# A sorted-expert feed-forward kernel: gathers paced by their own landings, and row transposes moved on VectorE

## The reference

```python
ys = cond_1024 / sqrt(512)
d = rsqrt(einsum('bi,io->bo', ys * ys, weight * weight) + 1e-8)
xf = einsum('bsi,io->bso', x * ys[:, None, :], weight) * d[:, None, :]       # conditioned input
top1 = argmax(softmax(xf @ gate_w.T), axis=-1)                               # one of 2 experts
masked = xf[None] * one_hot(top1).T[:, :, None]
h = relu(einsum('end,edh->enh', masked, w1) + b1[:, None, :])                # experts
routing = (einsum('enh,ehd->end', h, w2) + b2[:, None, :]).sum(axis=0)
shared = relu(xf @ sw1 + sb1) @ sw2 + sb2                                    # shared network
out = x + routing + shared
```

## Time and profile before

| | |
|---|---|
| median of 3 runs | 1408.37 us (1406.78 to 1408.86) |
| the profiled execution, its own time | 1408.37 us |
| span of that execution in the trace | 1406.6 us |
| PE busy | 1367.4 us (97%) |
| DVE busy | 1004.5 us (71%) |
| ACT busy | 679.7 us (48%) |
| POOL busy | 364.2 us (26%) |
| DMA, mean over the span | 238 GB/s |

### The profile page before, as it was taken

How to read it: one execution, slowest core, us unless ns; L and a number is a source line. 1 busy time by engine, 2 the same in 40 slices (tenths; PEclk the granted TensorE clock), 3 DMA queues, 4 the chain that set the end, 5 groups by cost and what they waited for, 6 DMA issues and landing times.

```text
span 1406.6 us, 17366 instructions
## 1 busy us (share of the span) xinstructions
PE 1367.4 (97%) x5990; PEld 1126.0 (80%) x5990; DVE 1004.5 (71%) x1424; ACT 679.7 (48%) x988; POOL 364.2 (26%) x328
## 2 busy tenths in 40 slices
PE   9999999999989999899999999999999999897997
PEld 7888888888868788787888888888888887785886
DVE  7979967667788967966557878777897758453331
ACT  4456644545455544665666444444564445231220
POOL 0000005544636544250000000000000032354884
PEclk9999999999999999999999999999999999998999
DMA  6967475776877578653668887978787899997762
GB/s 206 285 244 223 181 250 189 252 231 251 268 257 260 209 255 272 229 181 129 213 224 281 262 281 251 290 254 272 258 250 244 273 291 320 290 298 178 215 163 33
DMA packets 243449, 334.54 MB, mean 238 GB/s; under 512 B 71760, under 2 KB 106576, under 8 KB 243088
## 3 DMA queue, kind: packets, MB, share of 16 engines
q1 hardware_dynamic: 216592, 299.58, 64.7%
q0 software_dynamic: 21248, 30.30, 9.8%
q10 hardware_dynamic: 5520, 3.54, 0.8%
HBM read 201.25 MB, written 149.29 MB: 249 GB/s over the span
## 4 chain that ended last, share of the span: by engine, by line
PE 86%; DMA 6%; DVE 4%; issue 2%; POOL 1%; ACT 1%; POOLq 0%; DVEq 0%; ACTq 0%; SPq 0%
PE bank L2015 39%; PE bank L2093 30%; PE bank L2122 8%; PE bank L1943 6%; DMA rows<-xf_scratch,quad_tab 1%; DMA y_rows<-x_rows,tab 1%; DMA hin<-hidden_scratch 1%; DMA out<-y_rows,tab 1%; DMA hin<-expert_hidden 1%; DVE vb L1512 1%; PE bank L2034 1%; DVE xw L1448 0%; DMA y_rows<-sorted_rows_out 0%; PE bank L2135 0%; DVE hl L1479 0%
## 5 line engine op out<-in xcount | busy, mean ns | idle before, releaser
L2015 PE MATMUL bank<-xw,w_hi 128*128 128x512 f32 x1792 | 555.9, 392 | 14.3 <-DVE vb L1512 12.2
L2093 PE MATMUL bank<-hl,w_hi 128*128 128x512 f32 x1344 | 414.4, 389 | 2.4 <-DVE hl L1479 2.2
L2015 PEld LDWEIGHTS bank<-xw,w_hi 128*128 128x128 f32 x1792 | 337.9, 189 | 86.8 <-DVE vb L1512 13.8
L1479 DVE TENSOR_TENSOR hl<-hin,hl 128x512 fp32r<-128x512 f32 x400 | 265.1, 686 | 197.5 <-ACT hl L1037 189.9
L1037 ACT CAST hl<-hin 128x512 fp32r<-128x512 f32 x400 | 244.6, 621 | 323.0 <-PE bank L2093 185.1
L2015 PE MATMUL bank<-xw,w_lo 128*128 128x512 f32 x896 | 350.4, 391 | 0.0
L2093 PEld LDWEIGHTS bank<-hl,w_hi 128*128 128x128 f32 x1344 | 251.8, 188 | 56.5 <-issue 3.5
L2093 PE MATMUL bank<-hl,w_lo 128*128 128x512 f32 x672 | 261.4, 389 | 0.0
L2015 PEld LDWEIGHTS bank<-xw,w_lo 128*128 128x128 f32 x896 | 169.3, 189 | 35.7
L1061 ACT ACTIVATE vb<-bank,b 128x512 f32<-128x512 f32 x192 | 130.2, 688 | 115.9 <-PE bank L2015 92.7
L882 POOL DMA_INDIRECT rows<-xf_scratch,quad_tab x128 | 129.6, 1012 | 150.4 <-PE bank L2015 105.2
(11 more groups left out here) (199 smaller groups left out, 1337.1 us busy)
## 6 DMA issues: line engine op xcount, KB each, us to landing
hin<-hidden_scratch SPq DMA_DIRECT2D x168, 512.0 KB
hidden_scratch<-vb SPq DMA_DIRECT2D x120, 512.0 KB
hidden_scratch<-vt SPq DMA_DIRECT2D x48, 512.0 KB
hin<-expert_hidden SPq DMA_DIRECT2D x32, 512.0 KB
w_new<-w_shared SPq DMA_DIRECT2D x52, 256.0 KB, 5.4
expert_hidden<-vb SPq DMA_DIRECT2D x24, 512.0 KB
ring<-x_cols SPq DMA_DIRECT2D x32, 256.0 KB
xf_scratch<-xo SPq DMA_DIRECT2D x32, 256.0 KB, 4.8
```

Source lines behind the costliest of these rows:

```text
L1479: nc.vector.tensor_tensor(hl[:, n % HL, 1, :], hin[:, n // 2 % LOADS, n % 2, :], hl[:, n % HL, 0, :].bitcast(F32), ALU.subtract).then_inc( ...
L2015: last = nc.tensor.matmul(up_bank(u, UP_BANK[c])[p][:], w[:, DOWN_W[c], pair, part], xw[:, c, x, k, :], start=(c in FRESH and n == 1), sto ...
L2093: last = nc.tensor.matmul(bank[p][:], w[:, DOWN_W[c], i, part], hl[:, n % HL, h, :], start=(i == 0 and q == 0), stop=(i == PAIRS - 1 and q ...
```

## The change

Three edits in the up stage.

1. POOL: gather j no longer waits for a count of PE's parts. Instead gathers 8, 16 and 24 each wait until the chunk before them has landed (`rows_sorted`); the first gather waits for `xw_lo` alone.
2. ACT: the cast of operand 0 (`block_hi(s, 0)`) waits for all four flips in place of two.
3. DVE, for blocks 4 to 7: flips 0 and 1 now open group 2 of the block before, flip 2 takes the place where flip 0 stood, flip 3 the place where flip 1 stood, and group 3 has none.

```diff
-GATHER_AT = [9 + 6 * j // 5 for j in range(JW)]
...
                 pool.wait_ge(xw_lo, STEPS * s)
                 for j in range(JW):
-                    pool.wait_ge(up_mm, PER_GROUP * GROUPS * (s - 1) + GATHER_AT[j])
+                    if j > 0 and j % (JW // FLIPS) == 0:
+                        pool.wait_ge(rows_sorted[j // (JW // FLIPS) - 1], DMA * JW // FLIPS * (s - BLOCKS + 1))
                     if (s - 1) * GROUPS == LOOSE_UP[0] and j == JW // FLIPS:
                         pool.wait_ge(loose_up_done, 2)
...
-                act.wait_ge(x_flip, FLIPS * s + (2 if c == 0 else FLIPS))
+                act.wait_ge(x_flip, FLIPS * (s + 1))
...
                 if g == 2 and s < UPS - 1:
-                    for i in range(FLIPS if s < BLOCKS - 1 else 0):
+                    for i in range(FLIPS if s < BLOCKS - 1 else 2):
                         flip(s + 1, i)
                 if more:
                     block_lo(s + 1, 0)
-                    if s >= BLOCKS - 1:
-                        flip(s + 1, 2)
-                        flip(s + 1, 3)
                     x_sum_of(s + 1, 0)
...
                 if g == 2 and BLOCKS - 1 <= s < UPS - 1:
-                    flip(s + 1, 0)
+                    flip(s + 1, 2)
                 add(u, vt1, 5, 4, 0)
...
                 if g == 2 and BLOCKS - 1 <= s < UPS - 1:
-                    flip(s + 1, 1)
+                    flip(s + 1, 3)
```

## The result

| | median | profiled execution | span | TensorE busy | TensorE idle |
|---|---|---|---|---|---|
| before | 1407.57 us (1404.79 to 1408.86, 4 runs) | 1408.37 | 1406.6 | 1367.4 | 39.2 |
| after | 1424.27 us (1419.37 to 1424.89, 4 runs) | 1425.69 | 1423.9 | 1370.1 | 53.8 |

The ratio is 1.0113, with a 95% interval of 1.0091 to 1.0135: the change makes the kernel slower by 1.1%, 17 us. The forecast was 1407.0 with a range up to 1423, so the measured median lies 1.3 us above the range, and the likeliest case was wrong.

The account below looks back on a forecast made before the run. TensorE, busy for 97% of the span, was taken as the bound, with at most 16.4 us of stops to win. Block ends changed by -0.3, -0.3, -1.0 and +0.2, so -1.4 from 1408.37: 1407.0 us, range 1393 to 1423.

Parts of the forecast that it names:

- the likeliest case: The prediction's own forecast for the whole kernel: 1407.0 us, its own range 1401 to 1412, chance 0.5.
- Start of the gathers: First gather of each block on POOL: gain 0 in block 3, 0.9 us earlier in blocks 4 and 6, block 5 unchanged.
- The pace on POOL: Gathers 1.31 us apart inside a chunk plus three landing waits W, making F earlier by 1.1 to 2.1 us.
- W: Landing wait on POOL, from a chunk's last gather issue until its landing is seen: taken as 3.7 us.
- F: Start of flip 3 on DVE, set by the last landing: forecast at 394.9, 475.5, 558.7 and 637.3 in blocks 3 to 6.
- The four last waits: Waits from last gather issue to flip 3 in blocks 3 to 6: 6.4, 4.6, 5.7 and 2.45 us, taken as unchanged.
- What a late F costs: At block ends, step 4 may start at F + 4.1 us and DVE's third addition ends at F + 11.3.
- The tail and the second stop: After flip 3, first sum 2.2 us later; PE stops at steps 4 and 6, 1.4 us clock loss partly hidden.
- Flips 0 to 2 cost nothing: On DVE, flips 0 and 1 opening group 2 cost nothing if rows are there; no DMA wait at flips 0 to 2.
- The sum: PE's lateness at the ends of blocks 3 to 6 changes by -0.3, -0.3, -1.0 and +0.2: -1.4 us.
- Slow landings: Rival: bursts queue deeper on POOL; W = 5.0 gives 1423, up to 1444; 11 us per us of W from 4.1; chance 0.23.
- Quick landings: Rival: W and last waits near 2.45 us, all PE block-end stops gone, 1392 us; chance 0.17.

Follow-up runs that it names:

- e1: Kernel before with the change's landing waits on POOL alone, flips and ACT's wait as before: 1421.30 us, ratio 1.0104.
- e7: Kernel before with gathers in bursts of eight set by PE's count (gathers 0, 8, 16, 24 at counts 9, 19, 29, 38): 1407.62 us, ratio 1.0002.
- The parts alone: e1 and e2, each the kernel before with only some of the change's edits: ratios 1.0104 and 1.0047.
- e2: Kernel before with the moved flips and ACT's longer wait alone, gathers still paced by PE's count: 1412.91 us, ratio 1.0047.
- e11: Kernel before with gathers at PE counts 7 + 8j/7 in place of 9 + 6j/5: 1395.13 us, ratio 0.9918.
- e9: Kernel before with gathers at PE counts 9 + 8j/7 in place of 9 + 6j/5: 1400.50 us, ratio 0.9952.
- e4: Kernel after with the three landing waits on POOL left out, so no pacing: 1473.16 us, ratio 1.0485.
- e13: Kernel after with one landing wait in place of three, at gather 24 for chunk 2: 1458.66 us, ratio 1.0369.
- e6: Kernel after with landing waits two chunks behind (gather 16 for chunk 0, gather 24 for chunk 1): 1471.99 us, ratio 1.0486.
- e8: Kernel before with one gather at every PE count (9 + j): 1410.65 us, ratio 1.0018.
- e10: Kernel after with one landing wait in place of three, gather 16 waiting for gathers 8 to 15: 1397.50 us, ratio 0.9945.
- e12: Kernel before with one landing wait at gather 16 in place of all PE counts, old flips: 1451.85 us, ratio 1.0324.

## Why the prediction failed, by its own steps

**Start of the gathers: right in kind, misread in block 3.** There the first gather is released by DVE's `xw`, as forecast, but at 337.84 in place of 339.8. Before, the cast ended at 338.83 and the gather's row names PE as releaser, so PE's count held it for another 1.0 us; after, the cast itself starts at 336.34 in place of 337.61. Those 2 us were a gain that I had at 0. In block 5 the side path, which the forecast took as the limit, no longer binds: gather 8 is released at 530.70 by the landing of the chunk before it.

**The pace on POOL: the failed step.** W was mis-sized: 3.7 forecast, 4.5 measured, and the interval inside a chunk 1.31 forecast, 1.43 measured. By the prediction's own formula that is 28 x 0.12 + 3 x 0.8 = 5.8 us a block. Block by block, from first gather to F: 58.6 for 55.1 forecast in block 3, 63.5 for 53.3 in block 4, 54.7 for 51.2 in block 6. W was built from 3.1 us for the bytes and 0.55 from there until the waiting engine went on. In the kernel after, at the twelve landing waits, the last packet of the gathers' queue ends 2.1 to 6.1 us after the chunk's last issue, 4.0 on the mean, and POOL goes on 0.6 to 1.1 us behind it, 0.8 on the mean. Less the 0.3 of an issue that is 0.5. So the second part was right and the time of the bytes was short by 0.9. Two causes can be seen. The readings were a little early: taken to the packet that completes each chunk's bytes, the 16 of the kernel before give 3.4, not 3.1. And they came from gathers paced at about 1.6 us; in e1, which has bursts and landing waits, the bytes take 4.1 us. How much of that is the burst is open, since in e7, with the same bursts and PE's count, the same reading gives 3.5 for the first three chunks of a block (3.2 before). The longest wait, to 461.04 in block 4, shows what the gathers meet. The DMA queues of the kernel after from 456 to 458 us, then from 459 to 461:

```profile
q1 hardware_dynamic: 384, 0.76, 99.2%
...
q0 software_dynamic: 8, 0.00, 0.7%
```

```profile
DMA packets 17, 0.03 MB, mean 16 GB/s; under 512 B 2, under 2 KB 2, under 8 KB 17
```

For 2 us SP's queue (q1) fills the 16 engines and the gathers' queue (q0) moves 8 packets; its last one ends at 460.0, and POOL goes on 1.0 us later. The four last waits, 2.45 to 6.4 with a mean of 4.8, stood in the prediction as mere ends; W = 4.5 is close to their mean. The 1.31 took a gather's own time, 1.01 us, from the paced kernel; after it is 1.109 on the mean of 128.

The Trainium skill's rule ("DMA: Bandwidth & Descriptors", section "Anatomy of one DMA — SWDGE (gpsimd) path") gave an estimate of 2.15 us. No landing wait here is that short: the twelve gaps go from 2.69 to 7.13 us, so W from 2.4 to 6.8.

**What a late F costs: right.** F comes at 396.4, 488.2, 574.3 and 656.5. Against the time at which PE wants step 4 (its start less its stop), that is 1.9, 1.1 and 2.5 us behind in blocks 3 to 5 where 0.1 behind, 2.3 ahead and 1.3 ahead were forecast. Step 4 starts at 400.56 = F + 4.1, as forecast to the tenth. The third addition ends at F + 11.5; 11.3 was forecast. Step 4 starts 4.12 us after F in all four blocks, so each late microsecond of F reaches PE.

**The tail and the second stop: the first as forecast, the second nearly absent.** After a stop at step 4 the clock is at the lower level for a while, and 24 multiplications take 407.79 - 400.56 = 7.2 us in place of 5.45. That is 1.8, not 1.4 (before, the 24 behind each of the three stops took 6.8 to 7.0 us, 1.3 to 1.5 more), and step 6 is then wanted just when the third addition is there. The clock loss hides the longer tail more fully than I said. The windows of the kernel after, behind the first block end and the first stop in group 2:

```profile
400.50:405.50 5.00, 4.94 (x14) 3.94 (x15) 4.93 (x5) 2.06 (x4) 4.39 (x5) 0.64 0.29 105
...
469.04:474.04 5.00, 5.00 (x15) 4.02 (x16) 1.78 (x3) 3.01 (x5) 2.27 (x3) 0.67 0.67 231
```

14 and 15 multiplications in 5 us, where 22 fit at 0.227 each, at a granted clock of 0.64 and 0.67. The stop of 1.92 us in block 6 has no such loss: from 660.6 to 665.6 the clock is 1.00 and 22 multiplications start.

**Flips 0 to 2 cost nothing: wrong in block 4.** Flips 1 and 2 waited 5.22 and 3.22 us, as the text warned for a longer W, and PE stopped for 4.7 us.

**The sum.** How late PE reaches step 6 is, at each block end, its start less the unhindered time (step 4's wanted time + 5.45). After: 407.98 - 399.94 = 8.0, 499.73 - 492.57 = 7.2, 585.82 - 577.17 = 8.7, and 2.8 in block 6: 26.7 us. The forecast had 6.0, 4.2, 4.6 and 0.2 = 15.0, and before it was 16.4. So the block ends give +10.3 in place of -1.4; group 2 of block 4 adds 4.7 and 1.6 of clock (7 x 0.227 behind the first stop). That is 16.6 of the 17.3 us of span.

**The rivals.** Slow landings is what happened, with W at 4.5, over the turning point of 4.1 that it named. By its 11 us for each of W it would give 1416, so 7.4 of the 17.3 us of span. The other 9.9 it didn't have: 6.3 are group 2 of block 4, and 3.6 are what is left of the slower issue inside the bursts after the earlier starts have taken some back; no run separates these two. Quick landings fell. The parts alone add up to 1.0104 and 1.0047, the whole is 1.0113: they probably overlap, since e1's stop at step 6 and e2's at step 4 can stand for the same lateness, though the intervals are wide enough for a plain sum. That the start of the gathers was not the limit, which I took from one row, was too narrow a view: e11 starts PE's counts two earlier and gains 11 us over before, where e9's pace alone gives 7.

## What to carry to other kernels

A wait for a DMA's completion put between bursts costs the full time from issue to seen (here 4.5 us, three times a block), while a count of the bounding engine costs only what it is set to (e7); price such a wait from bursts under the same load, not from paced transfers. Ask of a removed wait what it paced: with none, e4 lost 4.9%. When a queue falls silent, look at what it waits for before you call it blocked (e4's stores). And before a pacing rule is exchanged for another, move its numbers: two constants in a list (e11) won 11 us where the change lost 17.

## What the runs showed of the hardware

Indirect gathers issued from POOL in long unbroken rows, most of them 1.25 us apart, bring DVE and ACT to a stand: their waits last up to 31.1 us (e13, DVE) and 23.6 us (e6, ACT) and end in events that the profile calls "remote", and PE then stops for up to 19.5 us (e4). SP's stores are late only because they wait for ACT's results (23.5 and 9.3 us in e4, 33.0 in e13). Paced by PE's count, at 1.48 to 1.57 us on the mean, 32 nearly in a row did not do it (e8), nor did 16 in e10, while 16 in e12 did, with the same instructions up to that point. What decides, and what it is that POOL's issuing takes from the others, stays open: no run here isolates it.

A landing is seen 0.6 to 1.1 us after the last packet of the gathers' queue has ended, at all twelve landing waits of the kernel after. The bytes themselves take 2.1 to 6.1 us from the last issue.
